# Second GCN layer's last product by token tiles, router product in three pieces, attention output added in DRAM

## What is computed

```
xn = layernorm(x)
# graph branch: A = adjacency with counts, plus the identity; dinv = deg ** -0.5
h  = dinv * (A^T (dinv * (xn + pos_encoding))) @ W1 + b1
h  = relu(batchnorm(h) * gamma + beta)
g  = relu(dinv * (A^T (dinv * h)) @ W2 + b2)
# linear attention, 16 heads of 64, 256 features
q, k, v = heads(xn @ Wq), heads(xn @ Wk), heads(xn @ Wv)
q', k' = relu(q @ proj), relu(k @ proj)
m  = (q' (k'^T v)) / (q' sum(k') + 1e-8) @ Wo + bo
x  = x + g + m
# mixture of experts: 8 experts, the best 2 of each token, softmax weights
y  = layernorm(x);  logits = y @ Wr.T
x  = x + sum over the 2 chosen experts of weight * ((y W1v) * silu(y W1g)) W2
```

## Time and profile before

| | us |
|---|---|
| median of 3 runs | 1661.7 |
| lowest, highest | 1661.55, 1662.3 |
| the profiled execution | 1660.71 |
| its span, first to last instruction | 1659.0 |
| PE busy in it | 1508.4 |
| from the end of H(2,7) to the first instruction on the logits | 59.6 |

### The profile page before, as it was taken

One profiled execution on the slowest core, in us unless ns is written; L12 is line 12 of the kernel. 1 busy time (PEld: TensorE's weight loads), 2 busy tenths in 40 slices (PEclk: granted clock), 3 DMA queues, 4 the chain that ended last, 5 costly groups with the idle time before them and its releaser, 6 DMA issues.

```text
span 1659.0 us, 21157 instructions
## 1 busy us (share of the span) xinstructions
PE 1508.4 (91%) x8316; PEld 1419.8 (86%) x8316; DVE 816.6 (49%) x1601; ACT 513.9 (31%) x587; POOL 153.3 (9%) x162
## 2 busy tenths in 40 slices
PE   3899999999999999799999899998996559999996
PEld 3889898989898989699999899998995459988885
DVE  6555757565565656612665223452345454544430
ACT  4233333333333342414221233221111224544441
POOL 0112020101010101000000000000000012223321
PEclk7999999999999999899999999999998759999998
DMA  9623131322222225648441043213333656676763
GB/s 290 209 31 52 60 43 60 40 63 37 64 36 66 46 57 127 248 117 220 138 107 47 26 116 94 85 32 83 108 106 108 236 131 180 170 204 173 197 150 73
DMA packets 72745, 183.63 MB, mean 111 GB/s; under 512 B 8987, under 2 KB 39823, under 8 KB 70927
## 3 DMA queue, kind: packets, MB, share of 16 engines
q1 hardware_dynamic: 52550, 135.17, 26.1%
q0 software_dynamic: 20096, 47.10, 15.4%
HBM read 124.15 MB, written 67.93 MB: 116 GB/s over the span
## 4 chain that ended last, share of the span: by engine, by line
PE 79%; ACT 6%; DVE 6%; DMA 4%; issue 3%; SPq 2%; POOL 0%; DVEq 0%; POOLq 0%; ACTq 0%
PE slot L1482 40%; PE slot L1539 11%; PE slot L1715 6%; PE slot L1725 6%; PE kvb L1715 3%; PE slot L1629 3%; PE slot L1620 2%; PE kvb L1597 1%; PE lsb L1583 1%; PE slot L1698 1%; DMA adj_d<-stage 1%; SPq L519 1%; DMA big_lo<-at_d 1%; PE slot L1583 1%; DVE kk_l L1226 1%
## 5 line engine op out<-in xcount | busy, mean ns | idle before, releaser
L1482 PE MATMUL slot<-big_hi,slab_h 128*128 128x418 f32 x1152 | 295.4, 365 | 33.0 <-DMA big_lo<-at_d 9.7
L1482 PE MATMUL slot<-big_lo,slab_h 128*128 128x418 f32 x1152 | 286.4, 357 | 0.0
L1482 PE MATMUL slot<-big_hi,slab_l 128*128 128x418 f32 x1152 | 283.8, 355 | 0.0
L1482 PEld LDWEIGHTS slot<-big_hi,slab_h 128*128 128x128 f32 x1152 | 213.0, 192 | 43.6 <-issue 19.4
L1482 PEld LDWEIGHTS slot<-big_hi,slab_l 128*128 128x128 f32 x1152 | 219.5, 191 | 3.6
L1482 PEld LDWEIGHTS slot<-big_lo,slab_h 128*128 128x128 f32 x1152 | 219.8, 191 | 3.2
L1539 PE MATMUL slot<-adj,xs_h 125*128 125x418 f32 x480 | 118.1, 354 | 0.8 <-DVE ztmp L988 0.5
L703 POOL DMA_DIRECT2D adj_d<-stage x80 | 67.7, 846 | 549.5 <-ACT stage L771 355.0
L1539 PE MATMUL slot<-adj,xs_l 125*128 125x418 f32 x480 | 117.4, 353 | 0.0
L737 POOL DMA_INDIRECT xg<-flat_d,token x32 | 31.2, 974 | 763.4 <-DVE token L1412 646.0
L988 DVE TENSOR_TENSOR slab_l<-slab_raw,slab_h 128x1024 fp32r<-128x1024 f32 x48 | 58.5, 1219 | 82.8 <-ACT slab_h L771 82.7
(11 more groups left out here) (286 smaller groups left out, 2489.7 us busy)
## 6 DMA issues: line engine op xcount, KB each, us to landing
slab_raw<-slabs_dram SPq DMA_DIRECT2D x48, 512.0 KB, 3.7
ws_raw<-w_dram SPq DMA_DIRECT2D x36, 512.0 KB, 5.8
adj_d<-stage POOLq DMA_DIRECT2D x81, 117.2 KB, 3.1
w_raw<-w_dram SPq DMA_DIRECT2D x9, 1024.0 KB, 4.8
adj_d<-eye_dram POOLq DMA_DIRECT2D x1, 6250.0 KB, 25.8
raw<-adj_d SPq DMA_DIRECT2D x3, 1828.8 KB
mix_d<-mixt SPq DMA_DIRECT2D x8, 627.0 KB, 4.0
mix_in<-mix_d SPq DMA_DIRECT2D x8, 627.0 KB, 4.0
```

The source lines that it names most:

```text
L1482: mm = ten.matmul(ps[:, 512 * q:512 * q + CW], w[a][:, kt, :], big[b][:, kt, CW * q:CW * q + CW], start=(kt == 0 and c == 0), stop=(kt == ...
```

## The change

Layer 2's last product is made by token tiles. W2 is loaded as 8 row tiles of 128 x 1024 (`rows_p`), the last six into places that the adjacency and the Z inputs leave, and all stay in SBUF. N(i) computes a 125-token tile at full width, 48 matmuls of 512 columns with the tokens of big as weights. DVE adds b2 (a broadcast tile `b2b`), takes the relu and adds `xm`, takes the layernorm statistics of the whole row, and LN2(i), FL(i) and FT(i) follow tile by tile; FT(i-1) stands behind N(i). The router product is done for tokens 0 to 499 behind FT(4), 500 to 999 and 1000 to 1249 at the end; each piece has its own transposes. The ranking (RK) is what RT was.

The attention output is transposed as it is made: OT(f-1) runs inside O(f), behind three eighths of its matmuls, OT(7) inside Z(1,0). DVE copies the block to `mixn`, and POOL adds it with an accumulating DMA to `xm_d`, a copy of x in DRAM that POOL made behind the adjacency add 40. `mix_d`, MA and otmp are gone.

Tiles 0 to 5 of the attention output are loaded once Q(7) is done; O(0) waits tile by tile. H(1,0) and N(0) start on Z(.,6), and wait for Z(.,7) before their last eighth. The expert weights' first loads wait for N(9).

```diff
+ROWS_AT = SLAB[("H", 2, 0)]
+CHUNKS = ((0, 4), (4, 8), (8, 10))
 # steps()
-        o += with_split(("O", f), {3: [("RP", 0), ("RP", 1)], 4: [("RP", 2)], 6: [("DG",)]}.get(f, []))
+        then = {3: [("RP", 0), ("RP", 1)], 4: [("RP", 2)], 6: [("DG",)]}.get(f, [])
+        o += with_split(("O", f), then + ([("OT", f - 1)] if f else []))
...
+            if layer == 1 and t == 0:
+                o.append(("OT", KD - 1))
             if t + 1 < KD:
                 o.append(("ZP", layer, t + 1))
+            if layer == 2 and t >= KD - 2:
+                o.append(("P", ROWS_AT + t - KD + 4))
+            if layer == 2 and t == KD - 1:
+                o += [("P", ROWS_AT + 4), ("P", ROWS_AT + 5)]
             o.append(("Z", layer, t))
...
+    o += [("P", ROWS_AT + 6), ("P", ROWS_AT + 7)]
+    for i in range(NT):
+        o.append(("N", i))
+        if i:
+            o.append(("FT", i - 1))
+        o += [("LN2", i), ("FL", i)]
+        if i == 5:
+            o.append(("R", 0))
+        if i == 6:
+            o.append(("RT", 0))
+    o += [("R", 1), ("RT", 1), ("FT", NT - 1), ("R", 2), ("RT", 2), ("RK",), ("PX",)]
 # places_of()
+        elif k[0] == "OT":
+            place[k] = 1 - turn
+        elif k[0] in ("R", "RT"):
+            place[k] = 2 + (k[0] == "RT")
 # SP
+                elif k == ("QE", PAIRS - 1):
+                    sp.wait_ge(psum_full, FULL[("Q", PAIRS - 1)])
+                    sp.wait_ge(att_stored, 32 * (PAIRS - 2))
+                    for t in range(PAIRS - 2):
+                        load_att(t)
+            sp.wait_ge(psum_full, FULL[("N", NT - 1)])
             for m in range(4):
                 load_ws(m)
 # POOL
+                if g == NG // 2:
+                    pool.dma_start(xm_d..., x...).then_inc(x_copied_out, 16)
...
+            pool.wait_ge(x_copied_out, 16)
+            for f in range(KD):
+                if f:
+                    pool.wait_ge(mix_added, 16 * f)
+                pool.wait_ge(dve_done, DVED[("OT", f)])
+                pool.dma_start(xm_d.rearrange("(j p) (f c) -> f p j c", p=T, c=128)[f], mixn[f // (KD - 1)][:, :, :],
+                               accum_op=ALU.add).then_inc(mix_added, 16)
 # ACT
+                    if layer == 1 and t == 1:
+                        act.wait_ge(mix_added, 16 * (KD - 1))
+                    part = n - ROWS_AT
+                    if part == 2:
+                        act.wait_ge(dve_done, DVED[("ZP", 2, KD - 1)])
+                    if part >= 2:
+                        act.wait_ge(psum_full, FULL[("Z", 2, KD - 2 if part < 4 else KD - 1)]) if part > 2 else None
+                        copy(rows_p[part][0], slab_raw[n % 2][:, :]).then_inc(act_done, 1)
+                        continue
 # DVE
                 elif kind == "OT":
                     f = k[1]
                     dve.wait_ge(psum_full, u)
+                    if 0 < f < KD - 1:
+                        dve.wait_ge(mix_added, 16 * f)
+                    dve.tensor_copy(mixn[f // (KD - 1)][:, :, :], blocks(ps, NT, 128, T)).then_inc(dve_done, 1)
+                elif kind == "N":
+                    tt(a_, ps[:T, 0:D], b2b[:, :], ALU.add).then_inc(dve_done, 1)
+                    dve.wait_ge(dve_done, DVED[k])
+                    dve.wait_ge(xm_landed[i % 2], LAND * (i // 2 + 1))
+                    link(dve.scalar_tensor_tensor(out=a_, in0=a_, scalar=0.0, in1=xm[i % 2][:, :], op0=ALU.max,
+                                                  op1=ALU.add))
+                    for q in range(2):
+                        ins = dve.bn_stats(l2st[:, i, 6 * q:6 * q + 6], a_[:, 512 * q:512 * q + 512])
 # PE
+            def mix_transposes(f):
+                free_slot(("OT", f))
+                ps = sums[SLOT[("OT", f)]]
+                ten.wait_ge(act_done, ACTED[("O", f)])
+                for j in range(NT):
+                    mm = ten.transpose(ps[:T, 128 * j:128 * j + 128], mixt[:, T * j:T * j + T], ident[:, :])
+                mm.then_inc(psum_full, 1)
 # PE, slab_product
+                    if k == ("O", 0) and kt < KD - 1:
+                        ten.wait_ge(at_landed[kt], 32)
+                    if k == ("H", 1, 0) and kt == KD - 1:
+                        ten.wait_ge(dve_done, DVED[("Z", 1, KD - 1)])
+                    if kt == 2 and k[0] == "O" and k[1]:
+                        mix_transposes(k[1] - 1)
 # PE
-                        ten.wait_ge(dve_done, DVED[("Z", k[1], KD - 1)])
+                        ten.wait_ge(dve_done, DVED[("Z", 1, KD - 2)])
+                elif kind == "N":
+                    if i == 0:
+                        ten.wait_ge(dve_done, DVED[("Z", 2, KD - 2)])
+                    for kt in range(KD):
+                        if i == 0:
+                            ten.wait_ge(dve_done, DVED[("P", ROWS_AT + kt)])
+                        if i == 0 and kt == KD - 1:
+                            ten.wait_ge(dve_done, DVED[("Z", 2, KD - 1)])
+                        for c, (a, b) in enumerate(COMBOS):
+                            for q in range(2):
+                                mm = ten.matmul(ps[:T, 512 * q:512 * q + 512], big[b][:, kt, T * i:T * i + T],
+                                                rows_p[kt][a][:, 512 * q:512 * q + 512], ...)
```

More of the change, by code:

```diff
@@ L133, in steps @@
                 o.append(("HT", KD - 1))
-        for f in range(KD):
+            if layer == 2 and t == 1:
+                o.append(("P", ROWS_AT + 1))
+        for f in range(KD if layer == 1 else 0):
             o += with_split(("H", layer, f))
-            if layer == 1 and f == 4:
+            if f == 4:
                 o.append(("ZP", 2, 0))
-            if layer == 1 and f:
+            if f:
                 o.append(("HT", f - 1))
[L140 to L149, removed]
+    o += [("P", ROWS_AT + 6), ("P", ROWS_AT + 7)]
[9 more added lines that the diff above has]
+    o += [("R", 1), ("RT", 1), ("FT", NT - 1), ("R", 2), ("RT", 2), ("RK",), ("PX",)]
     return o
@@ L231, in build @@
 def build(nc, x, src_cols, dst_cols, dst_groups, slabs, w1, w2, wr, proj, feat_rows, consts, turns, tie,
-          iota, keys, eye, pe, blank, before, places, tokens, out):
+          iota, keys, eye, pe, blank, before, places, tokens, b2_rows, out):
     ctx = ExitStack()
@@ new lines, in _ @@
+                        load_att(p)
+                elif k == ("N", 0):
+                    sp.wait_ge(psum_full, FULL[("Z", 2, KD - 1)])
+                    sp.wait_ge(dve_done, DVED[("Z", 2, KD - 1)])
+                    sp.dma_start(b2b[:, :], b2_rows).then_inc(b2_landed, 16)
+                    sp.wait_ge(mix_added, 16 * KD)
+                    for i in range(2):
+                        load_xm(i)
+                    sp.dma_start(tie_t[:, :], tie).then_inc(const_in, 16)
+                    sp.dma_start(place_iota[:, :], iota[:, 0:CAP]).then_inc(lists_in, 16)
+                    sp.dma_start(before_t[:, :], before).then_inc(lists_in, 16)
+                    sp.dma_start(place_no[:, :], places).then_inc(lists_in, 16)
+                    sp.dma_start(tok_t[:, :, :].rearrange("p j c -> p (j c)"), tokens).then_inc(lists_in, 16)
@@ L1359, in _ @@
             dve.wait_ge(dve_done, DVED[("PX",)])
+            for s in range(NFL):
+                dve.wait_ge(flat_stored[s], LAND * NT // NFL)
             rounds = dve.value_load(rounds_n[0:1, 0:1], min_val=1, max_val=ROUNDS)
@@ L1514, in _ @@
                         mm.then_inc(x_full, 1)
-                if kind not in PSUM_KINDS and kind not in ("KV", "S"):
+                if kind == "OT" or kind not in PSUM_KINDS and kind not in ("KV", "S"):
                     continue
@@ L1536, in _ @@
                     for j in range(NT):
+                        if layer == 1 and t == 0 and j == 2:
+                            mix_transposes(KD - 1)
                         for a in range(2):
@@ L1642, in _ @@
                 elif kind == "RT":
-                    ten.wait_ge(act_done, ACTED[("R",)])
-                    for j in range(NT):
+                    a, b = CHUNKS[k[1]]
+                    ten.wait_ge(act_done, ACTED[("R", k[1])])
+                    for j in range(b - a):
                         mm = ten.transpose(ps[:T, 2 * EXP * j:2 * EXP * j + 2 * EXP], lgt[:, T * j:T * j + T],
@@ L1790 @@
         "w1": w1,
+        "b2_rows": np.tile(f(L0_gnn_b2).reshape(1, D), (T, 1)),
         "blank": np.zeros((CAP, D), np.float32),
```

214 lines of the change are left out of this document (97 added, 117 removed).

## The result

The changed kernel takes 1704.7 us (median of 4 runs, 1702.6 to 1706.9) against 1661.6 for the kernel before in the same job: ratio 1.026, interval 1.0245 to 1.0276. It is slower, and 81 us above the forecast. The rival "slow adds, the other side" is what happened.

What follows compares the result with a forecast made beforehand. TensorE, busy 91% of the 1659.0 us span, was taken as the bound. Terms -43.5 -6.8 -9.7 +11.0 +2.4 +3 +5.5 = -38.1 took 1661.7 to 1623.6 us; range 1611 to 1643.

Steps and rivals of the forecast that it cites:

- slow adds, the other side: Rival in O: its period becomes an add plus about 3 us, costing 7 x (A + 3 - 15.4); chance 0.06.
- Most of the 3.1 is start-up, the same for any size, so I take 9.: Adds to xm_d in O: each takes 9 us, and up to about 12 us hides in a period of 15.4.
- 3 for all the O stage: Waits in O for adjacency work, slots and DMA engines shared with the adjacency loads: cost 3 us, from 0 to 8.
- The copy: Copy of x to xm_d behind add 40: takes 18 us, makes add 41 land near 387, costs 5.5, from 0 to 10.
- O(0): Start of O: attention tiles loaded earlier, PE goes on without the hole, O(0) ends at 706.8, not 716.5; gain 9.7.
- H(1,0), N(0): Starts behind Z(1,6) and Z(2,6): no hole over 3 us; H(1,0) gains 6.8, N(0) ends at t0+12.0.
- DT: Late in O, DT waits for OT(5)'s copy behind DG's chain: hole at most 4.1, taken as 2.4.
- The tail: From the end of Z(2,7), t0, to the router's logits: t0+143.3 instead of t0+186.8, gain 43.5.
- the slices with 7 and 5 tenths: Granted clock of the kernel before: it falls to 7 and 5 tenths in slices covering about 1260 to 1345 us.
- turns sign at 17.8: Adds in O: by the slow adds formula, an add of 17.8 us eats the whole gain.
- products, transposes, starts and tail: Products bring no gain; 80 transposes moved into O(1) to O(7) and Z(1,0) cost 11.0; starts gain 6.8 and 9.7, tail 43.5.

Runs made afterwards that it cites:

- the split: The changed kernel with each of the eight adds issued as two, rows 0 to 111 and rows 112 to 124; 1645.3 us, ratio 0.991 to the kernel before.
- The last kernel: Changed kernel with xm_d in blocks (5120 B adds), own buffer for f = 1, x copied in two pauses, adjacency loads held until add 0 landed; 1616.5 us, 0.973.

## Why the prediction was wrong

**The step that failed** is "Most of the 3.1 is start-up, the same for any size, so I take 9." An add measured 23.5 in the middle (17.0 to 32.0). The bounds written beside it, 3.1 to 31, held the value; the choice between them was the fault, and with it the 0.06 for the rival. The number of pieces was counted right, but which engines they go to was not asked: the adjacency add's 125 pieces used all 16, and these 1250 used 5. At 112 pieces per us the data alone is 11 us, nearly the whole of what a period of O hides, and the issue (3.64 us on POOL, 0.87 for the earlier trace rows) comes on top. In an add with no loads beside it the first piece moved 4.2 us behind the issue and the last 12.3 later, and it landed at 17.0.

The other 6 us of the middle one go with the loads beside it: the first piece moved 10.1 and 8.6 us behind the issue in the second and third add, and 4.2 in the fourth and fifth.

The mechanism was named correctly in the rival. Its formula, 7 x (23.5 + 3 - 15.4) = 78 on top of 1623.6, gives 1701.3 for 1704.7 measured. That it comes so near is partly luck: PE's holes add up to 68.3, and the formula has no term for the clock. With 17.0 for every add the same formula gives 1656, a small gain; so by it, and not by a run, the loads beside the adds decided the sign.

**A place that the sum had at 3 for all the O stage**: add 0 runs beside the adjacency loads, because `adj_complete` releases both. It landed in 32.0 us, and still in 23.8 with the split, in 16.75 with long pieces and in 15.4 with a tenth of the data. The sum named it ("the adds share the DMA engines with the adjacency loads") inside the 3; with a quick add it costs 9 to 22 us.

**The copy**, 5.5 forecast: 6.5 in the trace, 7.1 by the kernel with the copy in the pause. The chain in adds 40, 41 and 42:

```profile
366.30 3.67 DMA adj_d<-stage
...
370.67 16.25 DMA adj_d<-stage
...
387.59 3.11 DMA adj_d<-stage
```

Add 41 landed at 386.9 (387 forecast), the copy in 19.4 us (18; the 14.5 "at the best rate" beside it follows from none of the rows named there, which give 20 and more). The line beside it said where the copy would be free: POOL was idle for 41.54 us ahead of add 40.

**O(0)**, 9.7: it started without a hole, waited 1.86 before its last eighth, and gained 9.6.

```profile
710.67 0.84 PE L1536 MATMUL slot<-big_hi,slab_h 128*128 128x418 f32 x3 [1.86 <-DVE big_lo L1020]
```

**H(1,0), N(0)**: no hole at either, as said; the kernel with these starts alone gave 1638.2 for 1638.4. **DT**: 2.79 for 2.4.

**The tail**, 43.5: PE's N(2) and N(3), from the chain:

```profile
1244.35 11.45 PE slot L1699 x48
...
1255.89 1.24 DVE acc L1020
...
1257.17 11.41 PE slot L1699 x48
```

The period is 12.82 (12.73 forecast), N(9) ended at t0+128.4 (129.1), and the logits came at t0+145.3 (143.3), gain 41.5. The 2 us are the last transposes and router piece, which ran at the lower clock (granted 0.50 from 1355.5 us on) and not at the full one I took:

```profile
1355.56 1.90 PE L1627 MATMUL slot<-ident,flat 125*128 125x125 f32 x8 [1.43 <-DVE flat L1023]
```

Eight transposes in 1.90, where the earlier trace rows had 1.05. The prediction also placed the slices with 7 and 5 tenths too early: by 41.5 us each they are 1286 to 1369, so most of the 5 lies behind the logits at 1322.09, where this change does nothing, and a 5 stayed.

**The sum without the two failures.** The forecast less its copy and its 3 us for the Os is 1623.6 - 5.5 - 3 = 1615.1. The last kernel, which has neither cost, measured 1616.5. So the arithmetic of products, transposes, starts and tail held within 2 us in total, and one DMA's duration outweighed all of it. Add 0's slow stretch beside the loads goes with the engines' packets (below), but no run here changed the sharing of engines without that of memory, so what the memory adds stays open.

## What to carry to other kernels

Before a DMA is put on a path where something waits for it, count not only its bytes and pieces but the engines its rows are dealt to, and price it from a row with the same shape, or build it from rows that divide well (112 + 13, or long contiguous pieces). When a choice lies between ends as far apart as 3.1 and 31 and the path turns sign at 17.8, the chance of the far side is not 0.06. Ask of every DMA issued on an event what else that event starts, and look for the pauses that a queue already has.

## What the runs showed of the hardware

- An accumulating DMA of 125 rows by ten 512 B pieces used 5 engines: 17.0 us with no loads beside it, 23.5 in the middle, and POOL's issue took 3.64 us or more. Split in 112 + 13 rows: 7.7 us, issue 2.5 for both. As 125 contiguous pieces of 5120 B: 7.3 us, issue 0.83. Stored and not added, on 5 engines and mostly in records of 4096 B: 14.3 us.
- Small pieces nearly stop beside large ones in another queue. Beside the adjacency loads (records of 16720 B, 1.03 us each, 16 per us) add 0 moved 5 data pieces and 11 short records per us from 746 to 750 us, one for each of the 16 engines; alone it is 112. Split on 16 engines it is up to 350 alone and mostly 12 to 31 beside them. The Trainium skill, "DMA: Bandwidth & Descriptors", "Queues, rings and completion order", says that each engine takes turns between queues packet by packet; a turn then lasts as long as the neighbour's packet, which fits these rates but was not tested with another packet size of the loads. In that case longer pieces carry more per turn, and the 5120 B pieces did get through in 17.0 us where the 512 B ones took 36.
- An add issued behind a 5000 KB copy in the same queue waited for nearly all of it (16.25 us for an add of 3.1). Beside this copy and the two of 1680 KB (records of 64000 B, 3.1 us each, and of 53760 B) loads in the other queue moved 0.7 MB in 12 us and not 4.4.
